# Attention and gated FFN on 8 cores: weights of pieces without matmuls, order of the start, place of the 1/std rows

## The reference

```python
x = x + _layernorm(_L0_attn_ref(_layernorm(x), Wq, Wk, Wv, Wo))
x = x + _layernorm(_L0_ffn_ref(_layernorm(x), w1, s1, w2, s2, h1, hs1, h2, hs2, w3, s3))

# attention: 16 heads of 64, hidden 1024, x is (2, 8192, 1024)
scores = einsum('bhqd,bhkd->bhqk', q, k) * 64 ** -0.5
w = sigmoid(scores); w = w / (w.sum(-1, keepdims=True) + 1e-6)
out = einsum('bhqk,bhkd->bhqd', w, v)            # then @ Wo
# FFN, 1024 -> 4096 -> 4096 -> 4096 -> 1024
h = silu(x @ w1 * s1) * (x @ w2 * s2)
h = gelu_erf(h @ h1 * hs1); h = gelu_erf(h @ h2 * hs2); y = h @ w3 * s3
```

## Time and profile before

| | us |
|---|---|
| median of 3 runs | 4594.48 |
| lowest and highest of them | 4590.83, 4785.37 |
| the profiled execution | 4595.01 |
| its span, slowest core (core 1) | 4593.5 |
| spans of the 8 cores | 4586.7 to 4593.5 |
| TensorE busy in it | 4402.3 (96%) |
| VectorE, ScalarE busy in it | 3159.3, 2886.4 |

### The profile page before, as it was taken

How to read it: one execution, slowest core, us unless ns; L and a number is a source line. 1 busy time by engine, 2 the same in 40 slices (tenths; PEclk the granted TensorE clock), 3 DMA queues, 4 the chain that set the end, 5 groups by cost and what they waited for, 6 DMA issues and landing times.

```text
span 4593.5 us, 66585 instructions; the slowest of 8 cores (4586.7 to 4593.5 us)
## 1 busy us (share of the span) xinstructions
PE 4402.3 (96%) x23032; PEld 1619.5 (35%) x23032; DVE 3159.3 (69%) x3213; ACT 2886.4 (63%) x3170; POOL 200.2 (4%) x385
## 2 busy tenths in 40 slices
PE   6999999988999999999999999999999999999997
PEld 2333333333333333333333333333333334444443
DVE  4667777656899999777888888778888884331011
ACT  2677777766588888765677777655777774212221
POOL 0000000000000000000000000000000000000000
PEclk8999999998999999999999999999999999999999
DMA  7343334355877777777766666778666668898885
GB/s 207 98 101 100 97 93 105 76 97 110 140 139 136 138 135 133 141 147 156 150 138 135 137 136 138 154 139 168 135 136 140 135 130 153 151 174 151 155 151 115
DMA packets 178181, 616.82 MB, mean 134 GB/s; under 512 B 17216, under 2 KB 56256, under 8 KB 127936
## 3 DMA queue, kind: packets, MB, share of 16 engines
q0 software_dynamic: 54432, 396.39, 50.0%
q1 hardware_dynamic: 123424, 216.18, 16.9%
HBM read 957.49 MB, written 51.38 MB: 220 GB/s over the span
## 4 chain that ended last, share of the span: by engine, by line
PE 85%; DVE 7%; ACT 4%; issue 3%; DMA 1%; DVEq 0%; ACTq 0%; SPq 0%; POOLq 0%
PE psF L912 36%; PE psS L445 11%; PE psO L463 11%; PE psF L871 8%; PE psF L358 5%; PE psF L339 5%; PE psF L963 5%; ACT wtil L77 3%; DVE acc L501 2%; PE psF L469 1%; PE psF L396 1%; DVE acc L502 1%; PE psF L786 1%; PE psF L720 1%; DVE rec L540 1%
## 5 line engine op out<-in xcount | busy, mean ns | idle before, releaser
L77 ACT ACTIVATE wtil<-psS,rk 128x1024 bf16<-128x1024 f32 x2048 | 2163.2, 1111 | 737.4 <-PE psS L445 637.7
L912 PE MATMUL psF<-fb,wring 128*128 128x512 bf16 x8192 | 1880.1, 380 | 2.8 <-DVE tmp L928 2.8
L912 PEld LDWEIGHTS psF<-fb,wring 128*128 128x128 bf16 x8192 | 749.6, 98 | 1082.2 <-issue 266.0
L501 DVE TENSOR_TENSOR acc<-acc,wtil 128x1024 f32<-128x1024 f32 x722 | 884.7, 1225 | 189.3 <-ACT wtil L77 128.7
L502 DVE TENSOR_TENSOR acc<-acc,wtil 128x1024 f32<-128x1024 f32 x722 | 884.6, 1225 | 76.7 <-DVE acc L501 1.4
L445 PE MATMUL psS<-qring,kring 64*128 64x512 bf16 x3072 | 476.4, 383 | 35.5 <-ACT wtil L77 35.1
L928 DVE SCALAR_TENSOR_TENSOR tmp<-tmp,psF 128x512 f32<-128x512 f32 x256 | 174.9, 683 | 483.0 <-ACT tmp L77 483.0
L463 PE MATMUL psO<-wtil,vring 128*64 128x512 bf16 x3072 | 483.7, 392 | 0.3 <-DVE oacc L565 0.3
L871 PE MATMUL psF<-ln,wring 128*128 128x512 bf16 x2048 | 457.3, 379 | 11.7 <-DVE tmp L882 11.0
L77 ACT ACTIVATE tmp<-psF,he 128x512 f32<-128x512 f32 x256 | 176.2, 688 | 326.1 <-PE psF L912 326.1
L74 POOL DMA_DIRECT2D wring<-wb x360 | 190.0, 528 | 3428.8 <-PE psS L445 2163.3
(11 more groups left out here) (110 smaller groups left out, 2357.5 us busy)
## 6 DMA issues: line engine op xcount, KB each, us to landing
wring<-wb POOLq DMA_DIRECT2D x360, 1024.0 KB, 9.6
kring<-K_sc SPq DMA_DIRECT2D x192, 256.0 KB, 4.8
vring<-V_sc SPq DMA_DIRECT2D x192, 256.0 KB, 6.6
xrb<-xr SPq DMA_DIRECT2D x64, 512.0 KB, 3.9
xTb<-xT POOLq DMA_DIRECT2D x18, 1024.0 KB, 11.5
K_sc<-kblk SPq DMA_DIRECT2D x16, 1024.0 KB, 5.8
V_sc<-vblk SPq DMA_DIRECT2D x16, 1024.0 KB, 13.4
io<-xT SPq DMA_DIRECT2D x24, 256.0 KB, 6.8
```

The source lines that it names most:

```text
L77: return self.emit("act", lambda e: e.activation(out, in_, func, **more), waits)
L501: d = E("dve", lambda e: e.tensor_tensor(dst, dst, wt[:, 0:1024], ALU.add), [sig[0]] + self.now("dve"))
L912: i = e.matmul(self.psF[bk][:], wt[:, ic * 128:(ic + 1) * 128], src[:, ic * QT:(ic + 1) * QT], start=(ic == 0), stop=(ic == NCH - 1))
```

## The change

- `put_off` with 0 ticks calls at once.
- Start: the first two xr tiles are loaded ahead of wv; statistics of the tiles 0 and 1 follow the fold of wk, 2 and 3 six K pieces; the fold of wv stands behind K piece 6 of 8; the R piece of block 0 stands after two V pieces; the statistics tiles 4 to 7 stand among the Q pieces, 8 to 11 leave the start.
- The K copies of block 0 are made by ScalarE.
- `Rb` has two buffers; the R piece is split into `r_a` (two diagonals), `r_b` (two matmuls, two diagonals) and `r_c` (two matmuls and the copy), all of weight 0. Those of positions 16 and 17 are inserted among the K pieces of block 15.
- Pieces without matmuls (statistics, row call, y, l, final) have weight 0. A list with weights of 0 alone is counted by pieces.
- Block 1 makes the statistics of eight tiles, then two blocks share eight; the last is made in block 13.
- The lags of the chain of tile 0 are 0 (before: 1 and 2); the others keep theirs.

```diff
     def put_off(self, ticks, fn):
 
-        self.steps.append((self.ticks + ticks, fn))
+        if ticks:
+            self.steps.append((self.ticks + ticks, fn))
+        else:
+            fn()
...
-        self.Rb = P("Rb", QT, F32, b + 161)
+        self.Rb = [P("Rb0", QT, F32, b + 161), P("Rb1", QT, F32, 24)]
...
         self.xr_tok = {}
+        for t in range(2):
+            self.load_r(t)
         toks["wv"] = [self.dma("sy", self.stgB[:, sl], self.wqkv["wv"][:, sl], f"ld_wv{i}")
                       for i, sl in enumerate(quarter)]
-        for t in range(2):
-            self.load_r(t)
         for src, dst in ((self.s1, self.s1b), (self.s2, self.s2b), (self.hs1, self.hs1b),
                          (self.hs2, self.hs2b), (self.ident, self.idt)):
             self.dma("sy", dst[:], src, "ld_c")
         self.c_ok = [self.dma("sy", self.s3b[:], self.s3, "ld_c")]
         self.w_ok["wk"] = self.fold(self.stgA, self.wbf["wk"], toks["wk"], 0)
+        for t in range(2):
+            self.stats_tile(t)
         toks["wq"] = [self.dma("sy", self.stgA[:, sl], self.wqkv["wq"][:, sl], f"ld_wq{i}", self.w_ok["wk"])
                       for i, sl in enumerate(quarter)]
         self.load_x(1, toks["wv"][-1:])
         items = self.proj_items(0)
-        for it in items[:4]:
+        for it in items[:6]:
             it.fn()
+        for t in range(2, 4):
+            self.stats_tile(t)
         self.w_ok["wv"] = self.fold(self.stgB, self.wbf["wv"], toks["wv"], 1)
-        for i, it in enumerate(items[4:8]):
-            self.stats_tile(i)
+        self.stats_rows(0, 4)
+        for it in items[6:8]:
             it.fn()
-        self.stats_rows(0, 4)
         self.vfree = [list(self.w_ok["wv"]), list(self.w_ok["wv"])]
         for i, it in enumerate(items[8:16]):
             it.fn()
+            if i == 1:
+                for r in items[16:19]:
+                    r.fn()
+            if i == 3:
+                self.w_ok["wq"] = self.fold(self.stgA, self.wbf["wq"], toks["wq"], 0)
+        for i, it in enumerate(items[19:]):
+            it.fn()
             if i % 2:
                 self.stats_tile(4 + i // 2)
-            if i == 3:
-                self.w_ok["wq"] = self.fold(self.stgA, self.wbf["wq"], toks["wq"], 0)
-        for i, it in enumerate(items[16:]):
-            it.fn()
-            if i % 2 and i < 8:
-                self.stats_tile(8 + i // 2)
-        self.stats_rows(4, 12)
+        self.stats_rows(4, 8)
...
-            d = E("dve", lambda e: e.tensor_copy(self.kblk[p][:, oc * BLK:(oc + 1) * BLK], self.psF[bk][:]),
-                  [t] + self.kfree[p])
+            kb = self.kblk[p][:, oc * BLK:(oc + 1) * BLK]
+            if pos == 0:
+                d = self.act(kb, self.psF[bk][:], AF.Copy, [t])
+            else:
+                d = E("dve", lambda e: e.tensor_copy(kb, self.psF[bk][:]), [t] + self.kfree[p])
...
-        def r_item():
-            bk, fw = self.bank()
-            for j in range(4):
-                tg = b * 4 + j
-                i, tw = self.idn % 2, self.dg_free[self.idn % 2]
-                self.idn += 1
-                d = E("dve", lambda e, i=i, tg=tg: e.tensor_scalar_mul(
-                    self.dg[i][:], self.idt[:], self.rv[:, tg:tg + 1]), self.c_ok + self.r_ok[tg] + tw)
-                t = E("pe", lambda e, i=i, j=j: e.matmul(
-                    self.psF[bk][:, j * 128:(j + 1) * 128], self.onesf[:], self.dg[i][:], start=True, stop=True),
-                    [d] + self.ones_ok + fw)
-                self.dg_free[i] = [t]
-            a = self.act(self.Rb[:], self.psF[bk][:], AF.Copy, [t] + self.rb_free)
-            self.give(bk, [a])
-            self.rb_ok = [a]
+        Rb = self.Rb[pos % 2]
+        rst = {}
+
+        def r_diag(j):
+            tg = b * 4 + j
+            i = j % 2
+            rst[j] = E("dve", lambda e: e.tensor_scalar_mul(self.dg[i][:], self.idt[:], self.rv[:, tg:tg + 1]),
+                       self.c_ok + self.r_ok[tg] + self.dg_free[i])
+
+        def r_mm(j, fw):
+            i, bk = j % 2, rst["bk"]
+            t = E("pe", lambda e: e.matmul(self.psF[bk][:, j * 128:(j + 1) * 128], self.onesf[:], self.dg[i][:],
+                                           start=True, stop=True), [rst[j]] + self.ones_ok + fw)
+            self.dg_free[i] = [t]
+            return t
+
+        def r_a():
+            r_diag(0)
+            r_diag(1)
+
+        def r_b():
+            rst["bk"], fw = self.bank()
+            r_mm(0, fw)
+            r_mm(1, fw)
+            r_diag(2)
+            r_diag(3)
+
+        def r_c():
+            r_mm(2, [])
+            t = r_mm(3, [])
+            a = self.act(Rb[:], self.psF[rst["bk"]][:], AF.Copy, [t] + self.rb_free[pos % 2])
+            self.give(rst["bk"], [a])
+            self.rb_ok[pos % 2] = [a]
...
-            items.append(Item(2, r_item))
+            items += [Item(0, r_a), Item(0, r_b), Item(0, r_c)]
...
-            if lag:
-                self.put_off(lag, small)
-            else:
-                small()
-            self.put_off(lag + 1, rstd)
+            self.put_off(lag[0], small)
+            self.put_off(lag[1], rstd)
...
+        lag = (1, 2) if q else (0, 0)
...
-            self.put_off(1, out)
+            self.put_off(lag[0], out)
...
-            self.put_off(2, copies)
+            self.put_off(lag[1], copies)
         for c in range(NCD):
-            items.append(Item(3, lambda c=c: y_item(c)))
+            items.append(Item(0, lambda c=c: y_item(c)))
...
-            items.append(Item(2, lambda c=c: l_item(c)))
+            items.append(Item(0, lambda c=c: l_item(c)))
...
-            items.append(Item(3, lambda c=c: item(c)))
+            items.append(Item(0, lambda c=c: item(c)))
         return items
 
 
     def merge(self, items, att, n):
 
-        total = sum(i.w for i in items)
+        alike = not any(i.w for i in items)
+        total = len(items) if alike else sum(i.w for i in items)
         done = made = 0
         for it in items:
             it.fn()
-            done += it.w
+            done += 1 if alike else it.w
...
-        spans = {b: (2, 4 + 4 * (b + 1), 4 + 4 * (b + 3)) for b in range(1, 13, 2)}
-        spans[13] = (1, 60, 64)
+        spans = {b: (2, 4 * b + 8, 4 * b + 16) for b in range(2, 14, 2)}
+        spans[1] = (1, 8, 16)
...
-                st = [Item(1, lambda t=int(t): self.stats_tile(t)) for t in part]
+                st = [Item(0, lambda t=int(t): self.stats_tile(t)) for t in part]
                 if not todo:
-                    st.append(Item(1, lambda r=rows: self.stats_rows(*r)))
+                    st.append(Item(0, lambda r=rows: self.stats_rows(*r)))
...
+            if b == NBLK - 1:
+                kept = [self.proj_items(NBLK), self.proj_items(NBLK + 1)]
+                for i, its in enumerate(kept):
+                    for j in range(3):
+                        items.insert(3 + 6 * i + 2 * j, its[j])
...
-        self.merge(self.proj_items(NBLK) + self.proj_items(NBLK + 1), self.att0_block(NBLK - 1), 16)
+        self.merge(kept[0][3:] + kept[1][3:], self.att0_block(NBLK - 1), 16)
```

More of the change, by code:

```diff
@@ L400, in q_item @@
             if b == 0:
-                d = E("dve", lambda e: e.tensor_mul(self.q0[:, oc * QT:(oc + 1) * QT], self.psF[bk][:], self.Rb[:]),
-                      [t] + self.rb_ok)
+                d = E("dve", lambda e: e.tensor_mul(self.q0[:, oc * QT:(oc + 1) * QT], self.psF[bk][:], Rb[:]),
+                      [t] + self.rb_ok[pos % 2])
                 self.q0_ok = [d]
@@ L406, in q_item @@
                 dst = (self.qst if pos < NBLK else self.qst8)[i]
-                d = E("dve", lambda e: e.tensor_mul(dst[:], self.psF[bk][:], self.Rb[:]),
-                      [t] + self.rb_ok + self.qst_free[i])
+                d = E("dve", lambda e: e.tensor_mul(dst[:], self.psF[bk][:], Rb[:]),
+                      [t] + self.rb_ok[pos % 2] + self.qst_free[i])
                 self.qst_free[i] = [self.dma("sy", self.Q_sc[b, oc], dst[:], f"st_q{i}", [d])]
             self.give(bk, [d])
-            self.rb_free = [d]
+            self.rb_free[pos % 2] = [d]
             if oc == NCD - 1:
@@ L803, in chain_items @@
             items.append(Item(8, lambda oc=oc: wo_item(oc), (q, WO0 + oc // 4), oc % 4 == 3))
-        items += self.ln_items(A, SQ, lambda: self.a_ok, 0, 1, lambda: [load(c) for c in range(4)])
+        items += self.ln_items(A, SQ, lambda: self.a_ok, 0, lag, lambda: [load(c) for c in range(4)])
         def y_item(c):
@@ L837, in chain_items @@
         items += self.ln_items(lambda c: self.y1b[:, c * QT:(c + 1) * QT],
-                               lambda c: self.y1sq[c][:], all_y, 0, 1, lambda: None)
+                               lambda c: self.y1sq[c][:], all_y, 0, lag, lambda: None)
         def l_item(c):
@@ L995, in load @@
                                     self.io_free[c % 4] + self.y_all[q])
```

(5 more changed lines are left out.)

## The result

| | before | changed |
|---|---|---|
| median of the first three runs, us | 4594.48 | 5081.68 |
| median of 19 runs each, us | 4652.27 | 4544.6 |
| lowest of the 19, us | 4590.83 | 4537.4 |

The ratio of the times is 0.9886, 95% interval 0.9862 to 0.9909. It leaves out executions disturbed by a lowered clock, which the medians include (all of the changed kernel's first three were such, and its first profile too, so another execution of it is shown from here on: slowest core 4545.1 us, clock 0.991). On 4594.5 us the ratio is 52 us less (42 to 63), or about 4542 us. The forecast was 4528, so a gain of 66.8. By the ratio the time lies inside the stated range (4508 to 4561), but about 14 us of the forecast gain did not come.

A forecast was written before the change was run, and what follows sets the result against it. TensorE's queue was taken as the bound, supplied by ScalarE's sigmoids and VectorE's evacuations. 16.0 - 1.0 + 31.4 + 7.0 + 8.4 + 5 = 66.8 us off 4594.5 gave 4528 us, range 4508 to 4561.

The forecast's parts named there:

- second R piece: Among block 15's Q pieces: moving it among K pieces removes its wait and slow matmuls; 7.3 us there, 7.0 overall.
- Chains of tiles 1 and 2: FFN chains after w12: y ends some 3 us earlier, waits on squares shrink, pairs of scores go; gain 5 us (0 to 9).
- The start: Before block 1: reordered loads, folds and statistics, K copies on ScalarE, bring block 1 to 96.9 us; gain 16.0 (8 to 20).
- chain of tile 0: Output projection to w12: with lag 0, sums, Ln and Exp come ahead of the batches; gain 8.4 us (3 to 14).
- the rival of 4538: Start: wq's load binds and lands 10 us later, so the start gains only 6 us; total 4538 us, chance 0.10.
- Block 1: R piece in parts saves 0.7 us, but eight statistics tiles and a row call are added; 1.0 us lost.
- Blocks 2 to 13: Weight 0 leaves every matmul piece just one batch, ending pairs of scores except at row calls; gain 31.4 us (22 to 41.6).
- block 15's part: Block 15: 2.1 us gained for the first R piece, less 2.4 paid for the moved diagonals.
- waits come back in the blocks: Rival: tiles put VectorE behind, each pair's 1.2 us returns as a wait on a bank; total 4561 us, chance 0.12.
- the tiles stop being hidden: Rival, blocks 1 to 13: 56 statistics tiles of 1.5 us each all land on the path; total 4611 us, chance 0.02.

The follow-up runs named there:

- start_only: Kernel before plus only the new block 0 order, K copies on ScalarE and moved statistics tiles, weights and lags as before: median core's span 4579.3 us against 4589.4.
- stats_w0: Kernel before with only the statistics tiles and row calls given weight 0: spans of 4552 to 4558 us on six cores, median 4557.0, 32 us less.
- lag0: Kernel before with only the lags of tile 0's chain set to 0: ratio 1.0017 (0.9984 to 1.0050); output projections to w12 82.7 us, 87.7 before.
- r_mid_only: Kernel before with only the R pieces of positions 16 and 17 moved among block 15's K pieces, two Rb buffers: ratio 1.0012 (0.9972 to 1.0051).
- inter: Changed kernel with wv and wq casts dealt one per K or V piece, 16 store buffers, copies one tick late: block 1 at 100.5 us, lowest run 4540.54.

## The experiments: where the rest of the forecast went

**The second R piece, 7.3 forecast, 2.4 found.** With the R piece gone the Q pieces run faster, and the eight store buffers `qst8` are wanted again before their stores have landed. On core 2 of the changed kernel, VectorE and then TensorE in the last merge:

```profile
915.31 0.69 DVE L435 TENSOR_TENSOR qst<-psF,Rb 128x512 bf16<-128x512 f32 x1 [3.94 <-DMA Q_sc<-qst]
```

```profile
917.88 0.64 PE L491 MATMUL psO<-wtil,vblk 128*64 128x512 bf16 x2 [3.83 <-DVE oacc L593]
```

VectorE stands 3.94 us before the ninth Q piece's multiplication. The accumulation `oacc` is queued behind it on VectorE, and TensorE waits 3.83 us for the bank that this would free. First test, 16 buffers instead of 8:

```diff
-        self.qst8 = [P(f"qst8_{i}", QT, BF16, 12 + i) for i in range(8)]
+        self.qst8 = [P(f"qst8_{i}", QT, BF16, (12 + i) if i < 8 else b + 32 + i) for i in range(16)]
                 i = oc % 2 if pos < NBLK else oc
+                if pos == NBLK + 1:
+                    i = 8 + oc
```

> The changed kernel with sixteen store buffers for the Q results of the last merge instead of eight, so that the second set of Q pieces never waits for a store of the first. Theory 1: VectorE's wait of 3.0 us on the store and TensorE's of 2.9 us behind it are gone, 4 us less up to the first output projection (947 instead of 951) and at the end. Theory 2 (VectorE's reciprocals bind the last merge, the store's wait only comes first): under 1 us.

No wait on a store is left, and the stretch takes 65.3 us in the median (65.3 to 65.7; 68.8 in the changed kernel). At the end the gain can't be told: the spans are 4530.5 to 4540.8, median 4535.5 against 4537.0, the lowest run 4538.91 against 4538.54. From w12 to the end this profile takes 3505.5 us instead of 3502.1, which eats up the 3.5 us.

Why do stores of 128 KB take so long? The DMA issues of core 2 between 870 and 935 us (KB each, median us to landing) show three weight loads of 1 MB issued on POOL just then, and V's store of 1 MB on the Q stores' own queue. The tile's own view (860 to 1000 us) gives the slowest landing of a Q store (least, median, most):

```profile
wring<-wb POOLq DMA_DIRECT2D x3, 1024.0 KB, 23.2
Q_sc<-qst SPq DMA_DIRECT2D x13, 128.0 KB, 8.7
...
V_sc<-vblk SPq DMA_DIRECT2D x1, 1024.0 KB, 34.3
```

```profile
DMA to landing us min/median/max: 1.7/4.4/31.8
```

The landings one by one say more. V's store is issued at 880.2 us and lands at 914.6. The eight Q stores issued between 883.4 and 911.4 land at 915.2 to 918.0, one after the other. It is so on all 8 cores: the first Q store lands 0.3 to 0.7 us after V's, which takes 31.1 to 35.2 us. So the Q stores come in behind V's, and what has to be explained is why V's takes so long. Two things could hold it: the weight loads, or its own size.

The first attempt put the three `load_w()` behind the last merge in the program:

> The changed kernel with the three first weight loads of the FFN ring issued behind the last merge instead of ahead of it. If their packets are what keeps the stores of Q from landing: no wait of VectorE on a store (0.5 to 4.9 us in the changed kernel), first Q matmul to output projection 65.3 us on every core as with sixteen buffers (66.2 to 71.7 in the changed kernel); the output projection may then wait for its weights. If the stores stand behind each other on the queue of SP: waits as before.

This run missed its aim: POOL's list had nothing before them, so the loads were issued no later than before. Waits on stores were 0 to 3.7 us and the stretch 66.3 us in the median (65.4 to 70.9), which does not tell the theories apart. The second attempt makes the loads wait for TensorE's fifth Q piece of the second set:

```diff
+        def late():
+            fn4()
+            self.wr_free = [self.now("pe") for _ in range(3)]
+            for _ in range(3):
+                self.load_w()
+        kept[1][7].fn = late
```

> The changed kernel with the three first weight loads made to wait for the fifth Q piece of the second set, so that they truly start later (moved behind the last merge without a wait they started when they did before, since POOL's list was free). If the weight loads are what keeps the first stores of Q from landing: stores in under 10 us instead of 28 to 32, no wait of VectorE on one, 65.3 us from the first Q matmul to the output projection on every core; if the store of V's 1 MB just ahead of them on the same queue is: waits of 0.5 to 4.9 us as before.

Core 2 of this kernel, the same view of the Q stores:

```profile
DMA to landing us min/median/max: 1.7/3.2/17.5
```

and in the view of DMA issues between 870 and 935 us:

```profile
V_sc<-vblk SPq DMA_DIRECT2D x1, 1024.0 KB, 12.2
```

With eight buffers as before, no core waits for a store and the stretch takes 65.3 us in the median (65.2 to 65.7). V's store lands after 12.1 to 13.7 us, and the first Q stores again 0.2 to 0.3 us behind it. So the weight loads are the cause, by way of V's store: they lengthen its landing, the Q stores behind it land late, and the buffers run out. Loads beside Q stores with no V ahead of them lengthen the landing too: the 17.5 us is a store issued 1.4 us after the first of the loads that were put off, and nothing waits for it. All this was there before the change (V's store 32.8 us, the slowest Q store 27.4 on that core), but there the R piece's wait and its slow matmuls put off the ninth Q store to 962.9 us, and the first had landed at 956.0. The Trainium skill (DMA: Bandwidth & Descriptors, Queues, rings and completion order) says that a DMA engine takes turns between the queues it has work for; nothing here shows single turns.

**Chains of tiles 1 and 2, 5 forecast, 0.6 found.** The sums wait as long as ever: 3.17 and 2.80 us before, 3.13 and 2.85 in the changed kernel (medians of 8 cores, tiles 1 and 2). Changed kernel, core 1, tile 1: ScalarE, and then TensorE.

```profile
1936.39 0.67 ACT L77 ACTIVATE tmp<-psF,he 128x512 f32<-128x512 f32 x1
1936.96 2.11 ACT L77 ACTIVATE wtil<-psS,rk 128x1024 bf16<-128x1024 f32 x2
1938.96 0.72 ACT L77 ACTIVATE fb<-tmp,hh 128x512 bf16<-128x512 f32 x1
1939.57 0.63 ACT L77 ACTIVATE y1b<-y 128x512 bf16<-128x512 f32 x1
1940.09 0.63 ACT L77 ACTIVATE y1sq<-y 128x512 bf16<-128x512 f32 x1
```

```profile
1940.97 3.57 PE L748 MATMUL psF<-y1b,onesb 128*128 128x512 bf16 x8 [3.14 <-DVE acc L530]
```

The last `y` is made at 1936.8 to 1937.5. TensorE falls idle at 1937.8. The copy and the square stand two ticks late in ScalarE's list, behind two sigmoids and a scaling, and are done at 1940.7. Making y sooner can't help: the releaser in the waits changed its name, not its size. Two tests. The old weights back in the changed kernel:

```diff
-            items.append(Item(0, lambda c=c: y_item(c)))
+            items.append(Item(3, lambda c=c: y_item(c)))
-            items.append(Item(0, lambda c=c: l_item(c)))
+            items.append(Item(2, lambda c=c: l_item(c)))
```

> The changed kernel with the old weights 3, 2 and 3 of the y, l and final pieces. Forecast: 5 us slower than the changed kernel from w12 to the end (3507 instead of 3502). Theory 1 (the weight moves the batches, not the wait on the last square): 0 to 1 us, and in both the sums of the chains of tiles 1 and 2 wait about 3 us.

w12 of tile 0 to the end: 3503.6 us against 3502.1. The sums wait twice, 5.6 us. So these weights are worth 0 to 1.5 us. This kernel also shows what they do: counted from w12 the last y of tile 1 ends at 904.0 us with the old weights and at 900.5 with the new, but TensorE has lost the same batches ahead of the sums and falls idle at 903.9 and 900.8. Of 3.5 us, y gains 0.4 on TensorE. And the copies one tick late instead of two, for the tiles 1 and on:

```diff
-            self.put_off(lag[1], copies)
+            self.put_off(1 if q else 0, copies)
```

> The changed kernel, copies and squares of the y pieces of tiles 1 to 3 put off by one tick instead of two. Theory 1 (what holds the sums is the place of the last square in ScalarE's list, behind two sigmoids, an erf and a scaling): the two waits of 3.1 us before the sums shrink to about 1, 4 us less at the end. Rival (VectorE's end of y holds them): waits as before, 0 us.

> Copies and squares put off by one tick, for an undisturbed profile: the sums of the chains of tiles 1 and 2 wait 1.7 us and less instead of 3.1 and 3.0, and w12 to the end takes 2 to 3 us less than 3502 to 3503.

The ratio to the kernel before is 0.9847 (0.9780 to 0.9913), lowest run 4533.93. On the four cores of the second run with a clock of 0.992 or more, the stretch takes 3494.4 to 3495.5 us (3501.4 to 3503.4 on the same four cores of the changed kernel). The waits of core 1, and its sums of tile 1:

```profile
PE psF L748 <- ACT y1sq L77: 1.6, 2, 0.8
```

```profile
1931.42 1.89 PE L748 MATMUL psF<-y1b,onesb 128*128 128x512 bf16 x8 [0.78 <-ACT y1sq L77]
```

So 4.4 us less of waits are 7 us and more less of time. The rest is the matmuls behind the waits: the eight at 1940.97 take 3.57 us at a granted clock of 0.50 (1.00 up to the wait), the eight at 1931.42 take 1.89 at 1.00. In tile 2 such a set goes from 3.37 to 1.89 us. On core 1 that makes 4.4 + 1.7 + 1.5 = 7.6 us, and its time from w12 to the end falls by 7.7. A wait of this size does not always cost it: before the change the set of tile 1 ran in 1.89 us behind its wait of 3.2 on six cores, and in 3.57 on two.

**The start, 16.0 forecast, 13.2 found.** Two readings stand against each other: the K copies on ScalarE carry the gain, or the order does. The changed kernel with those copies on VectorE:

```diff
-            if pos == 0:
-                d = self.act(kb, self.psF[bk][:], AF.Copy, [t])
-            else:
-                d = E("dve", lambda e: e.tensor_copy(kb, self.psF[bk][:]), [t] + self.kfree[p])
+            d = E("dve", lambda e: e.tensor_copy(kb, self.psF[bk][:]), [t] + self.kfree[p])
```

> The changed kernel with the K copies of block 0 on VectorE again, in the new order. If the copies on ScalarE carry the gain of the start: block 1 begins 4 to 8 us later than 99.4 (copies of K 0 to 2 behind the fold of wk and two statistics tiles, K 6 and 7 behind the fold of wv). If the order of folds and tiles carries it: within 2 us of 99.4.

Block 1 begins at 98.8 (97.5 to 101.1; the seven profiles with ScalarE's copies have 98.6 to 99.4), the spans end at 4538.7: no difference. TensorE does wait 3.51 us ahead of the fourth K piece, for a bank that a K copy frees, but the fold of wv begins sooner (51.3 against 52.8 us in the median), since ScalarE has its casts done 10 us earlier. Core 1 of this kernel:

```profile
39.39 6.69 PE L346 MATMUL psF<-xTb,wkb 128*128 128x512 bf16 x24 [3.51 <-DVE kblk L351]
```

```profile
49.79 8.86 DVE L297 SCALAR_TENSOR_TENSOR wvb<-psS,stgB 128x2048 bf16<-128x2048 f32 x4
```

The same core of the changed kernel, VectorE and then TensorE:

```profile
53.23 1.29 DVE L316 BATCH_NORM_STATS2 bns<-xrb 128x6 f32<-128x512 f32 x2 [7.84 <-DMA xrb<-xr]
...
54.74 8.86 DVE L297 SCALAR_TENSOR_TENSOR wvb<-psS,stgB 128x2048 bf16<-128x2048 f32 x4
```

```profile
30.80 13.25 PE L346 MATMUL psF<-xTb,wkb 128*128 128x512 bf16 x48 [2.56 <-DVE wkb L297]
...
59.35 2.73 PE L368 MATMUL psF<-wvb,xTb 128*128 128x512 bf16 x8 [2.86 <-DVE wvb L297]
...
63.86 3.46 PE L368 MATMUL psF<-wvb,xTb 128*128 128x512 bf16 x8 [1.78 <-DVE rk L328]
...
81.14 7.07 PE L368 MATMUL psF<-wvb,xTb 128*128 128x512 bf16 x32
...
88.05 13.98 PE L424 MATMUL psF<-xTb,wqb 128*128 128x512 bf16 x64
```

Six K pieces run as one, V 4 to 7 end at 88.1 and the Q pieces follow at once at full clock, as worked out. But VectorE waits 7.84 us for a late xr load again, as before the change, and the fold of wv now stands behind it. It begins at 54.74 where the forecast had 50.9. That wait is only part of these 3.8 us, as the casts on ScalarE and the last of their sums on TensorE show (same core):

```profile
44.64 7.66 ACT L77 ACTIVATE wvb<-stgB 128x1024 bf16<-128x1024 f32 x8
```

```profile
52.45 0.59 PE L289 MATMUL psS<-wvb,onesb 128*128 128x512 bf16 x2 [0.35 <-ACT wvb L77]
```

The casts begin 2.1 us later than forecast (42.5), because the K pieces begin 0.9 us later (30.80 for 29.92) and six take 13.25 us instead of 11.8. The sums end at 53.0, and 1.7 us from there to the fold are the late tile's. Over the 8 cores the sums end at 51.9 in the median (forecast 50.8) and the fold begins at 52.8; the tile's load holds it for 0.8 to 1.7 us on five cores and not at all on three. V 0 and V 1 are late by as much as the fold, and V 1, after its wait, takes 3.46 us for eight matmuls. Last, the casts of wv and wq dealt one to each K and V piece, with 16 buffers and the earlier copies in it too:

```diff
+        for i, it in enumerate(items[:8]):
+            it.fn()
+            cast(i)
+            if i:
+                sums(i - 1)
```

> The changed kernel with three things: sixteen store buffers, copies put off by one tick, and the casts of wv and wq dealt out one to a K or V piece (ScalarE is idle 1.1 us of each 1.7 there), their sums one piece later, the statistics of tile 3 behind the fold of wv. If the folds' casts are what the start still waits for: wv is folded 5 us sooner, wq's eight casts no longer stand alone, block 1 begins near 90 instead of 99.4, and 9 + 5 + 3 us give 4522 in all. If wq's load binds: block 1 not before 96.

Block 1 begins at 100.5, 1.1 later than in the changed kernel and 1.3 later than in the next one, which differs from it in the start alone (99.2). Neither the 90 nor the 4522 us expected came: the lowest run is 4540.54, and TensorE's waits for the folds replace the ones taken away (core 1, 28 to 102 us):

```profile
PE psF L406 <- DVE wvb L334: 5.6, 2, 4.7
PE psF L462 <- DVE wqb L334: 2.5, 1, 2.5
```

**The two findings together**, 16 buffers and copies one tick late:

> The changed kernel with sixteen store buffers and copies put off by one tick. 2.5 to 3.5 us from the buffers, 7 from the tick (w12 to the end 3495 instead of 3502 where the clock holds in the chains of tiles 1 and 2): 4530, and 0.986 of the kernel before.

The ratio to the kernel before is 0.9841 (0.9792 to 0.9890), lowest run 4533.12. By the point it beats the changed kernel (0.9886) by about 20 us, but by its lowest run by 4, and the intervals overlap: better is likely, not shown. Against the earlier copies alone (0.9847, lowest run 4533.93) the buffers show nothing at the end. The stretch with the Q pieces is 65.3 us in the median (65.2 to 65.7). From w12 to the end it is 3494.4 to 3496.0 on three cores and 3503.0 to 3503.7 on three others, because there a load of `xT` comes late in the chain of tile 2, by 3.4 to 3.6 us. The two cores between (3498.4 and 3500.3) have no such wait, and what they lose is open. Core 0, VectorE (2850 to 2910 us) and TensorE (whole span):

```profile
DVE y L844 <- DMA io<-xT: 3.4, 1, 3.4
```

```profile
PE psF L750 <- ACT y1sq L77: 4.8, 2, 4.1
```

The changed kernel has the same wait in its slowest core, 5, where it costs more: 7.8 us of VectorE on `io`, 9.8 of the sums, and this core ends at 4545.1 where the others end at 4532.3 to 4538.9. The new weights of the y, l and final pieces bring it about, as profiles taken for other reasons show: after w12, with the old weights (the kernel before, `start_only`, `stats_w0`, `lag0`, `r_mid_only` and `ylf_back`) none of 48 cores waits for `xT`, with the new ones (eight kernels) 20 of 64 do, by 0.2 to 9.3 us at a time. `ylf_back` differs from the changed kernel in these weights only. In `inter` four cores wait 8.0 to 9.4 us, which is the other part of why it misses its aim. So these weights, worth 0 to 1.5 us in the median, can cost the slowest core of a run several. Why the load is late on some cores only is not shown.

## Why the prediction was right and wrong, step by step

The mechanism of the largest part, the weights of the pieces without matmuls, was right in kind and in size. Four terms of the sum were put too high, and in each a step failed that is named below: the second R piece (7.3, measured 2.4), the later chains (5, measured 0.6), the chain of tile 0 (8.4, measured 5.0) and the start (16.0, measured 13.2).

- **Start, 16.0, measured 13.2.** The order of the steps came out as worked out: six K pieces in a row, casts under them, V 4 to 7 straight into Q, wq's load not binding (the rival of 4538 for that reason falls). Mis-sized is "The wv casts now stand behind those copies: 42.5 to 50.2 (7.67 us), sums to 50.8, the fold 8.89 us to 59.8". The fold begins 1.9 us late in the median (52.8 for 50.9), of the 2.5 us by which block 1 is late (99.4 for 96.9). Two things are in it. The six K pieces take longer than I had them, so that the sums end at 51.9 for 50.8. And I costed the fold by its suppliers on ScalarE and TensorE and did not put tile 3, which stands before it on VectorE and whose xr load had been late in the very same profile: 0.8 to 1.7 us on five cores. On core 1 the two are 2.1 and 1.7. The copies on ScalarE, which I took to be what frees TensorE, are worth nothing beside the new order; with the old order they were not run.
- **Block 1, -1.0, measured -1.0.** Right.
- **Blocks 2 to 13, 31.4; with block 15's part 31.1, measured 33.1.** Right, and the count through merge was the whole of it: 50.2 and 51.6 where 50.25 and 52 were forecast. The rival "waits come back in the blocks" falls by this, and "the tiles stop being hidden" by block 3: four tiles, 50.20 us, TensorE busy for 50.20. The Trainium skill (ScalarE: Activation LUTs, What ACT_TABLE_LOAD costs) adds a drain of 1.38 us to each load. The blocks with a row call are 1.4 us longer than those without, all told, so the trace did not agree here either.
- **Second R piece, 7.3, measured 2.4.** The wait on `dg` and its slow matmuls went as forecast. The step that failed is "**Gain 7.0** (4 to 9.4)", which takes the whole removed wait as gain. What I left out is what becomes late next: I named the bank of PSUM that the R piece holds, and not the eight buffers that the freed Q pieces fill sooner. VectorE waits 0.5 to 4.9 us for one of them; with that wait away (two kernels, 16 buffers or later weight loads) the stretch is 65.3 us, a gain of 5.9. The stores' landings of 27 us stood in the trace of before and cost nothing there.
- **Chain of tile 0, 8.4, measured 5.0.** Mean, Ln and Exp do come before the batches. Up to the first sums 4.4 us are gained (26.5 to 22.1; forecast 2.2), from there to the second sums 0.7 are lost (33.9 to 34.6; forecast 30.4), and 1.2 are gained up to w12 (forecast 2.8). So the first part gave 2.2 us more than forecast, which hides some of what failed. The step that failed is "Ln at 1026.8, sigmoids from 1029.4", 4.4 and 7 us behind the start of the sums. On core 1, TensorE, VectorE, and ScalarE:

```profile
975.69 3.63 PE L748 MATMUL psF<-asq,onesb 128*128 128x512 bf16 x16
```

```profile
980.26 0.69 DVE L762 SCALAR_TENSOR_TENSOR lnr<-psF,lnr 128x512 f32<-128x512 f32 x1
```

```profile
981.03 1.28 ACT L77 ACT_TABLE_LOAD   x1 [3.60 <-DVE lnr L762]
982.32 0.72 ACT L77 ACTIVATE lnr<-lnr,epsl 128x512 f32<-128x512 f32 x1
```

  The table load stands behind the wait for `lnr`, with ScalarE idle for 3.60 us before it (on all 8 cores). I had hidden it in that idle time. Ln starts 6.6 us behind the start of the sums, and the sigmoids at 985.08, 9.4 us behind. That is 2.4 of the 4.2 us lost between the sums. Another 1.2 are ScalarE's wait for scores after the first two batches (1.23 us on core 1), which the forecast did not have; the last 0.6 are open. VectorE now waits for `xT` in this chain as well (2.8 to 4.8 us by core, not at all before), but ScalarE, the bound here, runs on without a pause.
- **Chains of tiles 1 and 2, 5, measured 0.6.** Failed at "y ends earlier by some 3 us, and of the 8.9 us that sums wait for squares in three places two of about 3 shrink". The first half is true by the clock (3.5 us in tile 1), but TensorE comes to the sums 3.1 us sooner as well, and the second half does not follow: the squares hang on a lag of two ticks in ScalarE's list, not on y. I took y for what makes the squares late, without looking at what they stand behind.
- **The sum.** All signs were right, and the largest term was right within 2 us. Four gains were put too high, by 2.8, 4.9, 3.4 and 4.4: 15.5, less the 2.0 that the blocks gained more, is the 13.5 between 66.8 and 53.3. In three of the four I followed the removed wait and did not ask what else stood in the same list, or came due, behind it. In the chain of tile 0 it was the table load's place in the list.

## What to carry to other kernels

A merge of two lists by weights should give weight only to pieces that feed the bound engine: a piece that costs TensorE nothing and counts 1 takes a batch away from one that would have covered it, and here that was 32 us of 52. When a stall is to be removed, list what the engine behind it will now want sooner (buffers with a store in flight, copies with a fixed lag, loads) and compare with the landing times in the same profile, waited for or not. A wait's named releaser is the last of its suppliers: before making that supplier faster, look in its engine's list at what it stands behind.

## What the runs showed of the hardware

- Eight stores of 128 KB, issued behind a store of 1 MB on the same queue, all landed after it: the first 0.3 to 0.7 us later on the 8 cores, up to 32.7 us after its issue. Others of 128 KB, in the same profiles, landed in 1.7 us.
- That store of 1 MB took 31.1 to 35.2 us beside three loads of 1 MB from another queue (23.2 us in the median on core 2), and 12.1 to 13.7 us when those were put off.
- A table load was not begun while the activation behind it had to wait: 3.60 us of idle ScalarE on each of the 8 cores, and only then the load's 1.28 us. Ln followed it 0.01 us later.
- Taking away 4.4 us of recorded waits on TensorE took 7 us off the time: the eight matmuls behind each ran at a granted clock of 0.50 in 3.57 us, and at 1.00 in 1.89.
